# Opening of a fused four-block transformer kernel: loads in pieces, and the first block's keys and queries in another order

## What is computed

```python
x = x + jnp.tanh(g_xattn[0]) * _L0_xattn_ref(_layernorm(x, axis=-1), ctx_1024, ctx_1024,
        L0_xattn_adj, mask_Bx1xSxS2_ik1, L0_xattn_Wq, L0_xattn_bq, ...)
# in it, with 16 heads of 8 features (batch B=4, S=256):
#   q = query @ Wq.T + bq;  k = key @ Wk.T + bk;  v = value @ Wv.T + bv
#   scores = q k / sqrt(8) + adj, masked;  softmax over keys;  times v;  @ Wo.T + bo
```

## Time and profile before

| | us |
|---|---|
| median of three runs | 754.45 |
| lowest, highest | 754.3, 762.99 |
| the profiled execution | 754.01 |
| its span, first to last instruction | 752.2 |
| TensorE busy | 691.6 (92%) |
| DVE busy | 541.8 (72%) |
| ScalarE busy | 487.7 (65%) |
| GpSimd busy | 215.1 (29%) |

### The profile page before, as it was taken

One profiled execution on the slowest core, in us unless ns is written; L12 is line 12 of the kernel. 1 busy time (PEld: TensorE's weight loads), 2 busy tenths in 40 slices (PEclk: granted clock), 3 DMA queues, 4 the chain that ended last, 5 costly groups with the idle time before them and its releaser, 6 DMA issues.

```text
span 752.2 us, 15037 instructions
## 1 busy us (share of the span) xinstructions
PE 691.6 (92%) x5030; PEld 374.0 (50%) x5030; DVE 541.8 (72%) x1717; ACT 487.7 (65%) x1343; POOL 215.1 (29%) x197
## 2 busy tenths in 40 slices
PE   6989997999999888998799999999989999889997
PEld 3655564656665223333156655663346656654332
DVE  4799999699996579488857999863066656546563
ACT  3888983689994776798658999626676556433111
POOL 2524651644353266266512233401000000000000
PEclk9999999999999879999899999999999999999999
DMA  5785000372000000000016200000000000000000
GB/s 205 160 273 227 3 2 1 95 154 70 3 1 2 1 0 1 0 2 0 1 21 128 44 3 2 30 1 0 0 1 1 1 1 2 1 1 0 1 0 28
DMA packets 19756, 27.59 MB, mean 37 GB/s; under 512 B 1504, under 2 KB 17760, under 8 KB 19040
## 3 DMA queue, kind: packets, MB, share of 16 engines
q1 hardware_dynamic: 19680, 26.64, 12.9%
HBM read 19.03 MB, written 7.60 MB: 35 GB/s over the span
## 4 chain that ended last, share of the span: by engine, by line
PE 66%; DVE 17%; ACT 10%; issue 5%; DMA 1%; DVEq 0%; POOL 0%; ACTq 0%; SPq 0%
PE bank L1133 12%; PE bank L1376 8%; DVE RING L1953 5%; PE bank L1538 4%; PE bank L1394 4%; DVE RING L1965 4%; PE bank L1236 4%; PE bank L1223 3%; PE bank L1325 3%; PE bank L1525 3%; PE bank L1432 2%; PE bank L1256 2%; PE bank L1752 2%; PE bank L1711 2%; ACT RING L846 2%
## 5 line engine op out<-in xcount | busy, mean ns | idle before, releaser
L932 ACT ACTIVATE RING<-RING,NMX 128x256 f32<-128x256 f32 x384 | 190.6, 500 | 25.4 <-DVE NMX L1953 23.3
L1953 DVE CUSTOM_DVE_ANT_0 RING<-bank,ADJM 128x256 f32<-128x256 f32 x384 | 145.4, 417 | 15.1 <-PE bank L1325 11.8
L1376 PE MATMUL bank<-W,RING 128*128 128x128 f32 x768 | 115.7, 282 | 6.6 <-ACT RING L944 6.3
L1376 PEld LDWEIGHTS bank<-W,RING 128*128 128x128 f32 x768 | 82.4, 141 | 49.0 <-ACT RING L932 35.2
L1965 DVE COPY RING<-bank 128x512 f32<-128x512 f32 x144 | 98.6, 686 | 5.0 <-PE bank L1376 4.6
L612 POOL TENSOR_TENSOR SUMS<-SUMS,small 128x8 f32<-128x8 f32 x36 | 59.2, 1643 | 125.3 <-ACT RING L932 125.3
L570 POOL TENSOR_TENSOR small<-small 128x2 f32<-128x2 f32 (+2 forms) x17 | 19.3, 1135 | 218.2 <-DVE small L1814 218.1
L932 ACT ACTIVATION_READ_ACCUMULATOR RING<-RING,NMX 128x1 f32 x384 | 73.1, 190 | 0.0
L846 ACT ACTIVATE RING<-bank,NMX 128x512 f32<-128x512 f32 x64 | 43.4, 683 | 42.3 <-DVE NMX L1882 22.6
L1882 DVE TENSOR_REDUCE NMX<-bank 128x1 f32<-128x512 f32 x64 | 39.4, 679 | 31.9 <-PE bank L1223 31.9
L1538 PE MATMUL bank<-ARENA,W 64*128 64x512 f32 x180 | 59.8, 671 | 2.5 <-DVE ARENA L2181 1.9
(11 more groups left out here) (272 smaller groups left out, 1257.8 us busy)
## 6 DMA issues: line engine op xcount, KB each, us to landing
ARENA<-scratch SPq DMA_DIRECT2D x12, 384.0 KB, 6.6
scratch<-ARENA SPq DMA_DIRECT2D x18, 192.0 KB, 2.7
W<-in_weights SPq DMA_DIRECT2D x1, 2564.0 KB, 22.5
ARENA<-scratch SPq DMA_DIRECT2D x12, 192.0 KB, 3.6
scratch<-ARENA SPq DMA_DIRECT2D x18, 128.0 KB, 6.6
W<-in_weights SPq DMA_DIRECT2D x2, 1024.0 KB, 13.8
W<-in_weights SPq DMA_DIRECT2D x1, 1905.5 KB, 14.9
scratch<-ARENA SPq DMA_DIRECT2D x18, 64.0 KB, 2.3
```

Of the source, the lines that this page charges most:

```text
L932: nc.scalar.activation(P_OF(n)[:, q * S:(q + 1) * S], S_OF(n)[:, q, :], ACT.Exp, bias=NMX[:, 2 * t + q:2 * t + q + 1], scale=-1.0, accum_o ...
L1376: mm = nc.tensor.transpose(bk[:, o:o + P], P_OF(n)[:, i:i + P], ident)
L1953: nc.vector.tensor_tensor_reduce(out=S_OF(n)[:, q, :], in0=SBANK(n)[:, q * S:(q + 1) * S], in1=ADJM[:, b, q, :], scale=-1.0, scalar=BIG, o ...
```

## The change

The columns of W are laid out anew, so that the identity, the gates, the bias columns, `wk0` and `wq0` come first (440 columns, `HEAD_W`). SP loads the first batch's x, these 440 columns and the first batch's context first, and the remainders of x, of CT and of the first piece of W afterwards, each with a semaphore of its own (`s_ldx2`, `s_ldc2`, `s_ldh`; `s_ld[0]` now stands for the remainder of W).

```diff
-            sp.dma_start(CT[:, :], ctxT_in).then_inc(s_ldc, 16)
-            sp.dma_start(W[:, 0:EDGES[1]], w_in[:, 0:EDGES[1]]).then_inc(s_ld[0], 16)
-            sp.dma_start(X[:, :, :], x_in).then_inc(s_ldx, 16)
+            sp.dma_start(X[:, 0:TPB, :], x_in[:, 0:TPB, :]).then_inc(s_ldx, 16)
+            sp.dma_start(W[:, 0:HEAD_W], w_in[:, 0:HEAD_W]).then_inc(s_ldh, 16)
+            sp.dma_start(CT[:, 0:S], ctxT_in[:, 0:S]).then_inc(s_ldc, 16)
+            sp.dma_start(X[:, TPB:NT, :], x_in[:, TPB:NT, :]).then_inc(s_ldx2, 16)
+            sp.dma_start(MASK[:, 0, :, :], mask_in[:, 0, :, :]).then_inc(s_ldm, 16)
             sp.dma_start(ADJ[:, 0, :, :], adj_in[:, 0, :, :]).then_inc(s_ldm, 16)
-            sp.dma_start(MASK[:, 0, :, :], mask_in[:, 0, :, :]).then_inc(s_ldm, 16)
+            sp.dma_start(CT[:, S:TOK], ctxT_in[:, S:TOK]).then_inc(s_ldc2, 16)
+            sp.dma_start(W[:, HEAD_W:EDGES[1]], w_in[:, HEAD_W:EDGES[1]]).then_inc(s_ld[0], 16)
...
 # GpSimd, key_parts: the wide keys are now the seventh and eighth to be emptied
-                pool.wait_ge(s_ek, (6, 10, 12)[a])
+                pool.wait_ge(s_ek, (8, 10, 12)[a])
...
 # TensorE, attention; ScalarE's copies are moved in the same way
                     if a == 0:
-                        first_keys(0, 0, NG)
-                        keys(0)
+                        first_keys(0, 0, 2)
...
-                    rehearse((1, 4, 3)[a])
+                    if a > 0:
+                        rehearse((4, 3)[a - 1])
                     turn(XN, 0, TPB)
-                    rehearse((2, 1, 1)[a])
+                    rehearse(1)
                     pe.wait_ge(s_ea, ra.n)
                     first_queries(a, 0, 2, rk, s_fk)
+                    if a == 0:
+                        first_keys(0, 2, NG)
+                        pe.wait_ge(s_ldc2, 16)
+                        keys(0)
...
                     if t == 4 and a == 0:
+                        pe.wait_ge(s_ld[0], 16)
                         values(0, 0, NC, rh, s_hf)
...
-            pe.wait_ge(s_ld[0], 16)
+            pe.wait_ge(s_ldh, 16)
+            biases()
             pe.wait_ge(s_ldc, 16)
-            biases()
...
 # DVE, attention
+                elif a == 0:
+                    normalise(X, XN, 0, TPB)
+                    dve.wait_ge(s_ldx2, 16)
+                    statistics(X, TPB, NT)
+                    first_masks()
+                    normalise(X, XN, TPB, NT)
...
                         if a == 0 and t == W8_T:
+                            dve.wait_ge(s_ld[0], 16)
+                            dve.wait_ge(s_gate, 1)
...
 # DVE, start of the program
-            chain(nc.vector.memset(HALF, -0.5))
-            settle()
-            nc.vector.tensor_copy(VE, HALF).then_inc(s_set, 1)
+            nc.vector.memset(HALF, -0.5).then_inc(s_set, 1)
+            dve.wait_ge(s_ldx, 16)
+            statistics(X, 0, TPB)
...
-            dve.wait_ge(s_ldx, 16)
-            dve.wait_ge(s_gate, 1)
             attention(0)
```

More of the change, by code:

```diff
@@ L66, in columns @@
     put("ident", P)
+    put("gates", 8)
+    put("cols", 48)
+    put("wk0", P)
+    put("wq0", P)
     put("ones", P)
@@ L70, in columns @@
     put("iota", NE)
-    put("gates", 8)
-    put("cols", 48)
     put("w8", P)
@@ L75, in columns @@
     for a in range(3):
-        put(f"wk{a}", P)
+        if a > 0:
+            put(f"wk{a}", P)
+            put(f"wq{a}", P)
         put(f"wv{a}", P)
-        put(f"wq{a}", P)
         put(f"wo{a}", PW)
@@ L101 @@
 COL, NCOL = columns()
+HEAD_W = COL["ones"][0]
 EDGES = [0, COL["wk1"][0], COL["wr1"][0], COL["wq3"][0], COL["wg"][0], NCOL]
@@ L331, in program @@
         s_ld = [sem(f"s_ld{i}") for i in range(len(EDGES) - 1)]
-        s_ldx = sem("s_ldx")
-        s_ldc = sem("s_ldc")
+        s_ldx, s_ldx2 = sem("s_ldx"), sem("s_ldx2")
+        s_ldc, s_ldc2 = sem("s_ldc"), sem("s_ldc2")
+        s_ldh = sem("s_ldh")
         s_ldcx = sem("s_ldcx")
@@ L954, in attention @@
                 ra.n += la.n
-            act.wait_ge(s_ld[0], 16)
+            act.wait_ge(s_ldh, 16)
             nc.scalar.activation(GATE, w("gates"), ACT.Tanh).then_inc(s_gate, 1)
@@ L1314, in attention @@
                         if j == 0 and g < 2:
-                            pe.wait_ge(s_ek, rk.n - 1 + g)
+                            pe.wait_ge(s_ek, 3 + g if a == 0 else rk.n - 1 + g)
                         elif j == 0:
@@ L1929, in attention @@
                     normalise(X, XN, 0, TPB)
-                    if a == 0:
-                        first_masks()
                     normalise(X, XN, TPB, NT)
@@ L2042, in top2 @@
                 nc.vector.tensor_tensor(SEL, SEL, SELB, ALU.add).then_inc(s_sel, 1)
-            chain(nc.vector.memset(HALF, -0.5))
-            settle()
-            nc.vector.tensor_copy(VE, HALF).then_inc(s_set, 1)
+            nc.vector.memset(HALF, -0.5).then_inc(s_set, 1)
+            dve.wait_ge(s_ldx, 16)
+            statistics(X, 0, TPB)
             at = COL["cols"][0] + CI["bq0"][0]
-            dve.wait_ge(s_ld[0], 16)
+            dve.wait_ge(s_ldh, 16)
             nc.vector.tensor_scalar(BQS, W[:, at:at + 3], float(DH) ** -0.5, None, ALU.mult).then_inc(s_bkq, 1)
```

## The result

| us | before | changed |
|---|---|---|
| runs of the first comparison | 762.99, 754.45, 754.3, 754.19 | 770.26, 768.24, 769.75, 767.1 |
| median | 754.38 | 769.0 |
| span of the profiled execution | 752.2 | 768.5 |
| its mean granted clock | 0.982 | 0.953 |

A forecast was written before the change was run, and what follows sets the result against it. The start of the first scores was taken to bound the kernel: root at 8.9 plus 7.4 gives 16.3 against 16.33 us, no gain. The forecast was 754.45 less 0.2, 754.2 us, range 749.3 to 755.6.

The forecast's parts named there:

- A shift of the first scores is a shift of the end: TensorE's loop, busy 28.31 of 29.00 us, runs without slack, so only the first scores' start, 16.33 us, counts.
- The switch holds the root (R = 8.9): GpSimd's opening code switch, at 1.5 us, takes 7.4 us, so the first reciprocal root begins at R = 8.9 us.
- my likeliest case: Opening: GpSimd's switch holds the root, first scores at 16.3 against 16.33 us, no gain; chance 0.48.
- R + 7.4: First scores begin 7.4 us after GpSimd's first root starts (R), with TensorE restarting at its slow rate.
- the switch does not hold the root: Rival: GpSimd's root begins at 4.2 us, first scores at 11.6; gain 4.7 us, 749.7 us; chance 0.22.
- The fetch: Opening loads: x lands at 3.05, first weights at 3.75, context at 4.0 us; TensorE begins at 3.75 instead of 7.00.
- From the root to the scores: Opening: XN at R + 1.4, then transposes, queries, last keys and wide products; scores at R + 5.9 fast, R + 7.4 slow.
- The rest at nothing: DVE's mask and remaining tiles, GpSimd's key parts and three extra DMA issues cost nothing; DVE cover 1.3 us.

The follow-up runs named there:

- e8: Changed kernel with one small root-like power on GpSimd straight behind the all-reduce of L658; one run, span 767.8 us.
- e9: Changed kernel with one more all-reduce, its output unread, as GpSimd's last instruction of the program; one run, span 767.8 us.
- e5: Changed kernel run again unaltered, beside more runs of the kernel before; ratio 0.9991, 752.34 to 769.64 us in 12 runs.
- e6: Changed kernel keeping its new loads and early statistics, but with keys, rehearsals and copies in the order of before; ratio 1.0085, 756.91 to 772.82 us.
- e11: Changed kernel with the heads of W and CT issued on ScalarE's queue instead of SP's; ratio 1.0109, 761.19 to 770.14 us.
- e4: Kernel before with two rehearsals dropped, leaving one as in the changed kernel; ratio 1.0144, 768.39 to 773.05 us.
- e12: Changed kernel unedited once more, beside the kernel before in the same call; ratio 1.0118, 760.97 to 771.23 us.
- e10: Kernel before, unedited, compared against itself with a second profile; 754.28 to 775.75 us, median 770.1 against 763.04 beside it.

## Why the prediction was wrong

**"A shift of the first scores is a shift of the end."** Late starts came through in full (4.2 and 4.4 us). An earlier one did not: I read from 28.31 us busy of 29.00 that the loop has no slack, but with F 1.98 us earlier TensorE's idle time in the first batch grew from 0.44 to 1.51 us. That part is small. What put the time outside the range is the silent second half, that nothing else moves the end. My sum held TensorE's speed constant because the clock read 1.00 over the opening. The trace of before already had 27.3 us at 1.2 GHz beyond 131 us, and by 0.404 these are 11 us of its 752. I never asked what these would be in another execution. The run of 762.99 us among the three was the hint; I took 0.44 us, the distance of two executions that had drawn alike, as the measure of repeatability, and built a range of 6 us for a kernel whose own times span 22.

**The switch holds the root (R = 8.9).** Wrong: the root began at 4.24 (9.45 in the earlier trace rows). The step of the argument that failed is the transfer from L650 and L666: those two switch to other code, the opening's switch finds its own there. The mechanism itself exists (e8, e9), and e9 is my likeliest case made real: R of 9.64 and F of 18.03, which is R + 8.4 where I had R + 7.4, since transposes and rehearsal took 2.01 us, not 1.74, the queries and last keys 3.57, not 3.0, and the wide products 1.71, not about 1.3. Had the changed kernel's first runs drawn S of 27 us, they would have measured about 752.3 us, as its fastest later one did. That lies inside my range, and would have been luck, with this step just as wrong. The rival "the switch does not hold the root" had the right opening and a chance of 0.22, with the gain put at 4.7 us; it is 1.95 at equal S.

**The fetch.** x landed 2.4 us after its issue and DVE read it at 3.11, as forecast (3.05). The head of W was put at 3.75 and came at 5.50 (4.59 in e5). The term mis-sized is the rate of the small loads: I took 0.26 us per 100 KB from 1120 KB in long rows, and 220 KB landed 3.43 to 4.33 us after its issue. The row of GB/s for the first 12 us (40 slices), of the changed kernel and then of the one before:

```profile
GB/s 0 0 0 0 0 27 164 185 167 241 321 264 116 109 147 181 261 323 225 283 294 270 225 300 314 420 396 482 435 479 425 452 384 384 442 397 455 417 434 430
```
```profile
GB/s 0 0 0 0 0 68 177 246 410 341 385 539 448 358 388 418 478 418 358 329 357 358 396 423 376 382 403 382 266 123 157 198 314 444 457 348 437 379 297 154
```

In the changed kernel it is 109 to 323 GB/s from 1.8 to 7 us, when the first x, the two heads (1 to 1.7 KB a partition) and the rest of x (3 KB) are under way, and 384 to 482 GB/s from 7.5 us on, with pieces of 2 to 7 KB a partition. Before, with CT and W in pieces of 4 and 8.75 KB a partition, it is 341 to 539 already from 2.4 to 5.4 us, so the low start is not one that every execution has. That the size of the pieces makes the difference fits both rows; no run changed it alone.

**From the root to the scores.** The sum for this rival had F at 11.6 with keys ending at 6.1; TensorE in fact started 1.8 us later and was at the slow rate until 9.81 (the one rehearsal L1164 took 1.28 instead of the 0.65 of the earlier trace rows), which together make 14.0 of the 14.19. In e5, with W at 4.59 and the rehearsal at 0.88, F is 12.53. Fetch and restart are thus what separates the forecast 11.6 from 12.5 to 14.2.

**The rest at nothing.** Held for the first softmax tile, for which DVE waits 2.51 us, and for the three more DMA issues on SP, which cost nothing that shows (e6, 0.2 us, standard error 0.5). It did not hold behind that: I asked of DVE and GpSimd only whether each is done in time, not what their instructions do to each other when the start moves, and that is where 1.1 us of e11's gain went.

**Still open.** Whether the change alters S is open: the means differ by 2.8 us with a standard error of 4.3, which is 1.1 us of span with one of 1.7. That error takes each run for a draw of its own, and they may not be: all four of the changed kernel's first runs, all four of e4 and five of six in e12, but also five of six in e10, have S above 60 us, where half of the 58 further runs of before have. A small effect of the order on S can hide in that. Why S differs between executions of one program is open too. Its work is the same each time; e10 shows TensorE busy all of 19.6 to 29.8 us at 0.50, where the profile of before has this work at 1.00.

## What to carry over

Read the mean granted clock of every run before comparing times: with it, S = 2 x (1 - clock) x span explained all but 0.9 us of a 23 us spread, and turned a verdict of "1.7% slower" into "2 us faster at equal S". If the times of a kernel come in several clusters, three runs in one of them are no baseline; measure the kernel against itself first. Busy time close to the span in one execution does not say that the loop keeps up with an earlier start. A wait seen later in a program (a code switch, here) is no proof of the same wait at its start, which depends on what the execution before left behind.

## What the runs showed of the hardware

- One program, unchanged, spends between 27 and 79 us of its span at TensorE's 1.2 GHz level, and each of these us lengthens the span by 0.404 us. This makes 11 to 32 us, 1.4 to 4.1% of the span. The Trainium skill, "TensorE: Matmul & The Clock Gate", Part 1, calls the length of the slow phase run-variable and puts the cost of the ramp under 1% of a typical span. The rehearsal L1164 took 1.28, 0.88 and 0.80 us in three executions of the changed kernel, which agrees with the first. The second is on the ramp at a kernel's start, and does not cover this case, where the clock falls again in the middle of the work.
- GpSimd's code switch held its instruction for 7.27 and 6.99 us inside the program in e8 (L658, L660), and for 7.6 and 5.8 us at L650 and L666 before. At the start of the execution it put the first root off by 5.4 us in e9, behind a program that ended with another instruction, and by nothing in the changed kernel; that the code left behind decides this is inferred.
- A DVE instruction on 128x4 elements took 0.70 to 0.81 us in the ten profiles in which a GpSimd TENSOR_TENSOR on 128x768 was running, and 0.17 us in the four in which none was.
- A 128 KB transfer took 2.4 us and a 220 KB one 3.4 to 4.3 us from issue to landing at an otherwise idle start.
